# Four chained attention layers over four images on one core: two chains of work mixed by fixed tables on every engine queue

## What is computed

```python
x = L0(x)   # full attention, queries and keys of 32 channels; out = gamma * (V @ attn^T) + x
x = L1(x)   # group norm, full attention over 256 channels, output projection, + x
x = L2(x)   # layer norm, CAUSAL attention of 8 heads of 32 channels with one shared key/value head,
            # output projection, layer norm, feed-forward (layer norm, w1, layer norm, gelu, w2)
x = L3(x)   # as L1, other weights
```

## Time and profile before

| | us |
|---|---|
| three runs | 1576.68, 1571.64, 1568.68; median 1571.64 |
| profiled execution, its own time | 1572.43 |
| its span, first to last instruction | 1570.7 |
| mean granted TensorE clock | 0.898 of 2.4 GHz |

### The profile page before, as it was taken

How to read it: one execution, slowest core, us unless ns; L and a number is a source line. 1 busy time by engine, 2 the same in 40 slices (tenths; PEclk the granted TensorE clock), 3 DMA queues, 4 the chain that set the end, 5 groups by cost and what they waited for, 6 DMA issues and landing times.

```text
span 1570.7 us, 21594 instructions
## 1 busy us (share of the span) xinstructions
PE 1326.2 (84%) x7440; PEld 999.4 (64%) x7440; DVE 1008.6 (64%) x1913; ACT 567.8 (36%) x777; POOL 122.8 (8%) x314
## 2 busy tenths in 40 slices
PE   5789888958978988984998898896798898889688
PEld 4568664547866865444876776544686687645577
DVE  2647568666565756866656565877575565696665
ACT  2324224514342423452434331452343242245143
POOL 0000011210000001121000000212000000112100
PEclk9789979989979987997998997998798899799699
DMA  4000110000000011000000003000000001100000
GB/s 140 1 27 1 41 42 2 2 1 1 29 1 27 1 44 39 2 1 1 1 29 1 27 0 82 2 1 1 1 1 29 1 1 38 45 1 2 1 1 27
DMA packets 16393, 27.20 MB, mean 17 GB/s; under 512 B 2576, under 2 KB 6800, under 8 KB 16272
## 3 DMA queue, kind: packets, MB, share of 16 engines
q1 hardware_dynamic: 16272, 25.66, 5.9%
HBM read 8.61 MB, written 4.19 MB: 8 GB/s over the span
## 4 chain that ended last, share of the span: by engine, by line
issue 88%; POOL 7%; PE 4%; POOLq 0%; DVE 0%; ACT 0%
PE ring L589 3%; POOL cprobs L560 3%; POOL rstd L544 2%; POOL idle_pool L559 2%; PE ring L670 0%; POOLq L426 0%; PE ring L738 0%; POOLq L543 0%; PE ring L743 0%; ACT h_hi L974 0%; DVE x L1174 0%; POOLq L547 0%; DVE gn_nb L1250 0%; DVE gn_msc L1249 0%; DVE gn_sc L1248 0%
## 5 line engine op out<-in xcount | busy, mean ns | idle before, releaser
L1030 ACT ACTIVATE cprobs<-ring 128x1024 f32<-128x1024 f32 (+1 forms) x192 | 152.1, 812 | 206.3 <-PE ring L855 205.8
L589 PE MATMUL ring<-probsT_hi,vt_hi 128*128 128x512 f32 x384 | 158.2, 412 | 11.9 <-DVE probsT_lo L1120 11.6
L918 ACT ACTIVATE probsT_hi<-ring 128x1024 fp32r<-128x1024 f32 x96 | 98.1, 1026 | 188.4 <-PE ring L670 188.0
L1120 DVE TENSOR_TENSOR probsT_lo<-ring,probsT_hi 128x1024 fp32r<-128x1024 f32 x96 | 116.5, 1221 | 67.0 <-ACT probsT_hi L918 67.0
L831 PE MATMUL ring<-ks,qs 96*128 96x512 f32 (+3 forms) x384 | 144.0, 452 | 17.9 <-DVE part_max L1375 6.1
L589 PE MATMUL ring<-probsT_hi,vt_lo 128*128 128x512 f32 x384 | 153.9, 401 | 0.0
L589 PE MATMUL ring<-probsT_lo,vt_hi 128*128 128x512 f32 x384 | 153.6, 400 | 0.0
L1375 DVE TENSOR_REDUCE part_max<-ring 128x2 f32<-128x1024 f32 (+3 forms) x128 | 127.3, 1017 | 35.1 <-PE ring L835 17.2
L855 PE MATMUL ring<-qs,ks 98*128 98x512 f32 (+3 forms) x384 | 115.6, 396 | 13.6 <-DVE part_max L1375 12.1
L544 POOL TENSOR_TENSOR rstd<-var_eps,half_neg 128x2 f32<-128x2 f32 (+1 forms) x52 | 46.2, 889 | 997.8 <-DVE var_eps L1245 548.1
L926 ACT ACTIVATE probs<-ring,neg_max 128x1024 f32<-128x1024 f32 x96 | 106.8, 1113 | 42.0 <-DVE neg_max L1154 38.8
(11 more groups left out here) (218 smaller groups left out, 2592.3 us busy)
## 6 DMA issues: line engine op xcount, KB each, us to landing
qs<-q_hi SPq DMA_DIRECT2D x64, 128.0 KB, 2.3
xin<-x_dram SPq DMA_DIRECT2D x4, 1024.0 KB, 5.1
qs<-q_lo SPq DMA_DIRECT2D x32, 128.0 KB, 2.3
out_dram<-x SPq DMA_DIRECT2D x8, 512.0 KB, 2.9
qs<-max_rows SPq DMA_DIRECT2D x64, 4.0 KB
raw_L_wv<-L_wv_dram SPq DMA_DIRECT2D x2, 256.0 KB, 6.2
raw_L_woT<-L_woT_dram SPq DMA_DIRECT2D x2, 256.0 KB, 6.3
raw_L_wq<-L_wq_dram SPq DMA_DIRECT2D x2, 256.0 KB, 6.6
```

Of the source, the lines that this page charges most:

```text
L589: ins = mm(out, w, m, start=first and n == 0, stop=last and n == len(every) - 1)
L918: A(dst, flat(name) if src is None else src, ACT.Identity, bias=bias, scale=scale).then_inc(hi_ready, 1)
L1030: A(causal_probs(step, two, n), slot(event_name(e))[:, :, 0:n], ACT.Exp).then_inc(act_read, 1)
L1120: ins = v.tensor_tensor(dst, src, f32(hi), ALU.subtract)
```

## The change

1. **Two chains.** The loop over images is gone; the program is written out. One chain holds the 12 full layers in the order of `FULL`, which shifts the images against each other; the other holds the preparation and the four causal layers. `weave` merges both chains on each engine by a table `ORDER` of one character per piece of work (for PE 1221 characters: F or a digit, the first PSUM bank, for the full chain; a letter for the causal one). The engines still run strictly in order.
2. **Values of full layers in plain fp32.** `probsT` and `vt` are no longer split; `turned` and `values` are one copy each on ACT, and the DVE steps `probsT_lo` and `vt_lo` are gone. The product is one fp32 matmul of 128 x 256 instead of three fp32r matmuls of 128 x 512: `full_values` works in quarters of 256 queries.
3. **Causal blocks of 256 queries.** 8 blocks per image instead of 4 (`BLOCKS`), one `exp` event for four heads. SP stacks the queries per block: 12 DMAs of 32 x 256 for each of 8 blocks, 96 per image instead of 24, and 32 for the maxima instead of 16.
4. PSUM is a ring of 7 single banks and one accumulator bank. Probabilities are scaled on DVE in all 12 full layers, as before.

The diff, cut to what the prediction speaks of:

```diff
-def causal_blocks():
-
-    return [(0, 0), (1, 0), (0, 1), (1, 1)]
...
+FULL = [("L0", 0), ("L1", 0), ("L0", 1), ("L1", 1), ("L0", 2), ("L3", 0), ("L1", 2), ("L0", 3), ("L3", 1), ("L1", 3),
+        ("L3", 2), ("L3", 3)]
...
+SCALED_BY = ["dve"] * len(FULL)
...
+ORDER = {
+    "PE": (
+        "0F2eF02F4Fg02F40Fg24F02FFF3F50F24FFF5F02e6FFF0c3FFF64F024F0F2404F20F42F06FFF4F20F46FFF2F04c6FFF06FFFec0F4F0c"
...
+BLOCKS = [(hg, qi) for qi in range(NQ) for hg in range(HG)]
...
+def weave(order, full, causal):
+
+    for ch in order:
+        next(full if ch in "F0123456" else causal)
...
-                    for a in range(4):
-                        for g, src in enumerate((q2[0], q2[0], q2[1])):
-                            sp.dma_start(qs[DH * g:DH * (g + 1), ib, a::4, :].bitcast(F32),
-                                         src[DH * a:DH * (a + 1), :, sl].bitcast(F32)).then_inc(stack_in[ib][a // 2], 16)
...
+                for g, src in enumerate((q2[0], q2[0], q2[1])):
+                    for a in range(4):
+                        sp.dma_start(qs[DH * g:DH * (g + 1), k % STACKS, a, :].bitcast(F32),
+                                     src[DH * a:DH * (a + 1), hg, token_quarter(qi)].bitcast(F32)
+                                     ).then_inc(stack_in[k % STACKS], 16)
+                    yield
...
+            def causal_chain():
+                for b in range(B):
+                    for k in range(STACKS):
+                        yield from stacks(b, k)
+                    yield from shifts(b, 0)
+                    yield from shifts(b, 1)
+                    for k in range(2, K):
+                        yield from shifts(b, k)
+                        if k + 2 >= STACKS and k + 2 < K:
+                            yield from stacks(b, k + 2)
...
-                    last = product(acc[:, ct, :], [([s[:, j, ct * P:(ct + 1) * P] for s in vt],
-                                                    [s[:, ib, j, :] for s in probsT])
-                                                   for j in range(j0, j0 + TPH)],
-                                   first=j0 == 0, last=j0 + TPH == NT)
...
+                        last = mm(o[:, ct * QUARTER:(ct + 1) * QUARTER], vt[:, j, ct * P:(ct + 1) * P],
+                                  probsT[:, qi % (NQ - 1), j, :], start=j == 0, stop=j == NT - 1)
...
-                    lo(b, f"{l}.t{ti}", ap[1], ap[0], slot(f"{l}.t{ti}").rearrange("p b (s n) -> p (b s) n", n=P))
...
+                nc.scalar.copy(probsT[:, ti // 2 % (NQ - 1), :, (ti % 2) * P:(ti % 2 + 1) * P],
+                               slot(name).rearrange("p b (s n) -> p (b s) n", n=P)).then_inc(read_done["f", "act"], 1)
```

More of the change, by code:

```diff
@@ L63, in attention_order @@
     else:
[L64 to L76, removed]
@@ L77, in attention_order @@
-    return out + last
-def causal_schedule():
[L93 to L117, removed]
+        out = [("gn", 0), ("q", 0), ("v", 0), ("v", 1), ("s", 0), ("s", 1), ("q", 1), ("v", 2), ("v", 3), ("s", 2)]
@@ L127, in causal_schedule @@
             step += 1
+        fill = fills(k, len(base))
         for i, e in enumerate(base):
             events.append(e)
-            events += [f for at, f in fill[k] if at == i]
+            events += [f for at, f in fill if at == i]
             if divide:
                 events.append(divide.pop(0))
[L133 to L136, removed]
@@ L139, in evenly, with is_final @@
[L139 to L148 removed]
+            if is_final(e):
+                divide += norm(e[1])
+    tail = NQ - 2
+    events += divide + pending + norm(K - 1) + [("tg", tail), ("w2", tail)]
+    return events + [(e, tail + 1) for e in FEED_FORWARD]
+def is_final(e):
+    return e[0] == "values" and e[2] == TPQ * (BLOCKS[e[1]][1] + 1) - 1
@@ new lines, in causal_name, with full_units, causal_banks @@
+    return f"C{b}." + ".".join(map(str, e[:4] + e[-1:]))
+FILLED_BY_ACT = ("xt", "shift", "exp", "tg", "w2")
+NO_UNIT = ("norm", "ln2b", "f1b", "f2b")
+def full_units():
+    out = []
+    for l, b in FULL:
+        for e in full_events(l):
+            out.append((full_name(l, b, e), "act" if e[0] in ("s", "t", "v") else "dve", 1 if e[0] in ("gn", "o") else 2))
+    return out
+def causal_banks(e):
+    if e[0] == "max":
+        return 1 if e[-1] == 2 and e[5] - e[4] <= P else 2
+    if e[0] == "exp":
+        return 1 if queries(e[1], e[2]) <= P else 2
+    return 2 if e[0] in ("xt", "xn", "q2") else 1
@@ new lines, in queries, with ring_places @@
+def queries(k, jt):
+    return QUARTER - max(jt * P - BLOCKS[k][1] * QUARTER, 0)
+def ring_places(order):
+    full, causal = ([u for u in units if u[2]] for units in (full_units(), causal_units()))
+    queues = {"0123456": iter(full), "abcdefg": iter(causal)}
+    place, previous = {}, {}
+    holder = [None] * RING
+    for ch in order:
+        for banks, units in queues.items():
+            if ch in banks:
+                at = banks.index(ch)
+                name, _, width = next(units)
+                place[name] = at
+                before = [holder[i] for i in range(at, at + width) if holder[i]]
+                previous[name] = sorted(set(before), key=before.index)
+                holder[at:at + width] = [name] * width
+    return place, previous
@@ new lines, in causal_exponents @@
+            def causal_exponents(b, e):
+                _, k, jt, step = e
+                n = queries(k, jt)
+                if jt == 0:
+                    pe.wait_ge(shift_in[k % 2], 64 * (K // 2 * b + k // 2 + 1))
+                name = causal_name(b, e)
+                open_unit(name)
+                for a in range(4):
+                    last = mm(heads(name)[:, a, 0:n], ks[0:3 * DH + 2, jt * P:(jt + 1) * P],
+                              qs[0:3 * DH + 2, k % STACKS, a, QUARTER - n:QUARTER], start=True, stop=True)
+                last.then_inc(filled["c"], 1)
```

1803 lines of the change are left out of this document (974 added, 829 removed).

## The result

| | before | changed |
|---|---|---|
| median of five runs, us | 1569.44 (1564.61 to 1576.68) | 1553.94 (1552.49 to 1558.38) |
| ratio, 95% interval | | 0.9907 (0.9879 to 0.9935) |
| profiled execution, own time / span | 1572.43 / 1570.7 | 1558.38 / 1556.6 |
| granted clock | 0.898 | 0.928 |

A forecast was written before the change was run, and what follows sets the result against it. PE was taken as the bound, though neither always at work nor at full clock. Its work of 1222 us plus 14 + 24 + 12 + 40 + 76 + 12 of losses gave 1400 us, range 1300 to 1500.

The forecast's parts named there:

- Values in fp32: Full layers' values on PE: 768 fp32 products at 0.432 us, 332 us, replace 261.5 us of split products, +70.
- SP's queue: Start of each causal layer: 48 stack DMAs delay the first exp to 37.5 us; +76 for stops, +12 for clock.
- rival A: SP's stop at the causal layers' starts does not happen; 1330 us, chance 0.25.
- DVE at 870: DVE's busy time falls from 1009 to 870 us without the low-part steps for values.
- the start: Kernel start: first product needs only L0's weights and the image, at 14 to 16 us; +14.
- L0 and L1 alone: Image 0's L0 and L1, with only the preparation beside them, keep losses of 20 and 4: +24.
- the last L3: L3 of image 3 runs alone: its 4, a group norm's delay of 4 and the final store 4, +12.
- What is left of the waits in the mixed part: Causal layers beside nine full layers: 4% of waits, +40; bounds 0 and 15% (150).
- About 0.1 us on each side: Causal values on PE: switching to narrow tiles and back, 0.19 us per event; 64 more events, +12.
- B: Mixed part: the two fixed orders trip over each other, 13% of waits instead of 4%; 1490 us, chance 0.15.
- C: Mixing hides almost nothing, all 431 us of waits stay and PE does 82 more; 1653 us, chance 0.05.
- That small sum is inside the losses: Full layers' values: 11.6 of 11.9 us of PE idle before values, put down to `probsT_lo`, counted within the losses.

The follow-up runs named there:

- grp2: The changed kernel with neighbouring pieces swapped in PE's order alone, so fewer changes between the two chains are left; 1613.96 us, ratio 1.0275.
- the unmixed table: The changed kernel's same instructions with the two chains not mixed: each causal layer, then its full layers; 1940.79 us, ratio 1.2358.
- before_hi3: The kernel before with three fp32r value passes, all from high parts, without DVE's subtractions, ACT writing turned tiles one exponent later; 1521.34 us, ratio 0.9656.
- the scratch: The changed kernel with queries sent through DRAM, so a stack is 3 DMAs per head group instead of 12; 1497.33 us, 0.9549 of the kernel before.

## Why the prediction was wrong

**Right.** *Values in fp32*: 0.216 per record, 332 us; and 77 us for the same columns in the kernel before (forecast 70). *SP's queue*: 37.5 us from queries to `exp` against 37.0 to 38.3, and 88 us for the stops with their clock against 92; rival A falls. That the sum fits so well is in part luck: the wait was put too high, 19 against 15 per image, and the clock too low, 3 against 7. *DVE at 870*, *the start* (first product at 14.3 us, 14 lost), *L0 and L1 alone* (27 for 24) and the last L3 (18 for 12) were near. PE's pieces are worth 1233 for 1222.

**Wrong: "What is left of the waits in the mixed part ... I take 4%, +40".** With the ends of the causal layers and what of the 103 was no stop (103 - 92), this term is 138 + 46 + 11 = 195 us. Of these, 22 are the masks' additions, which the prediction had priced as work; the other 173 are still beyond its upper bound of 150. Four things are in them.

- *I read idle time as loss.* The 4% were derived from the stretch of 40 us in the earlier trace rows with 7% idle. The same piecewise reading of that stretch would have said it: its products' columns are worth 32.7 of the 40.9 us from whole group to whole group, 20% less than the time. A busy PE is not PE at its price. In the four quiet windows of the changed kernel more than half of the 108 lost us are busy time. Some 20 are at the 156 values events of the causal layers, which cost 50 where my prices held 30; 15 stand beside waits, since the record of the last matmul ahead of a wait runs on beyond its columns (0.28 us where 256 columns are worth 0.12); 12 are the masks' additions and 9 half clock.
- *The way into and out of the causal values was read too short.* "About 0.1 us on each side" took in what the earlier trace rows show up to the end of the event; the first product behind it pays 0.1 us more. An event costs 0.34 us beyond its columns (50 us for 148 ways in and out), not 0.19, so the 64 additional events of the smaller blocks are +22, not +12, and all 160 together cost 24 us more than my prices held. That it is the narrow tiles, and not plain fp32, fits the values of the full layers, plain fp32 of 128 columns, whose changes cost nothing; no run varied the width.
- *The base for the causal chain was wrong.* I took its latencies from the kernel before (191 us alone, 73 of them waits) and set 285 us of room beside them. The causal layer of 256-query blocks takes 245 alone. Image 3's, which I had put at 200 to 220, took 256, about what it takes by itself, although PE has only 184 us of work there.
- *The ends and starts of causal layers have waits of their own*, 46 us for the feed-forward alone, where the other chain has no piece at the right place. The order decides this, and grp2 shows how tightly: a swap of neighbours costs 56 us.

The sum again, with what was measured: 1211 of pieces + 14 + 27 + 92 for the stops + 195 in the mixed part + 18 = 1557, the span.

**The rivals.** B ("the two fixed orders trip over each other", 13% of 1018 us, 1490) came nearest in mechanism and size: the mixed part loses 17% (173 of 1018) without the stops, though part of this is no wait of one chain for the other. I gave it 0.15 and took it for a rare case, because in my count half of the loss was invisible. C's base of 431 us was too small: unmixed, the new pieces lose 708, so the mixing hid over half of it. Of the 384 us that it hid, 277 are above the old 431, brought along by the change itself; the unmixed table, which overlaps less at the end of L1 than the kernel before, is part of that.

**DVE's low parts.** "That small sum is inside the losses" held the 11.6 us behind `probsT_lo` and overlooked the 15.0 behind `vt_lo` and the 15.0 behind the scaling; before_hi3 gained 51 us. In the kernel before this worked for the fp32 values, +26 instead of +77; how much of it the mixed kernel keeps, no run shows.

**What stays open.** No run varied the block size alone, the width of the causal values or the ends of the causal layers, and none tried an order planned with SP's real issue time. That such an order would regain more than the scratch does is argued, not shown.

## What to carry to other kernels

Before a wait is given to a better interleaving, price the busy time too: set the work by its start-to-start prices against the clock on the wall of the very stretch that serves as the model, and not its idle share. When a change replaces the pieces as well as their order, measure the new pieces unmixed; the waits of the old ones say nothing about them. And a queue that only issues DMAs belongs in the plan of a fixed order like an engine: here 48 issues of 0.64 us at four places cost some 90 us, and three DMAs instead of twelve gave 59 back.

## What the hardware showed that I had not expected

- SP issued a DMA within SBUF in 0.62 us, with 32 KB as with 128, but the twelve from the DRAM scratch, 128 KB each, in 5.53, 0.46 each. The size did not matter within SBUF; whether the scratch as source or the shape of the transfer makes the difference, no run tells apart.
- Going into the 32-wide causal values costs PE 0.12 to 0.15 us beyond the columns and coming out of them some 0.22 (0.17 ahead of transposes), and the profile counts it as busy. Changes between other groups of matmuls, from 96 to 128 rows, from fp32r to plain fp32 or from one chain to the other, have a median of 2 ns.
- Work taken off PE was given back in part by the clock: with 240 us less of it, PE's busy time fell by 217 and the granted clock from 0.928 to 0.906.
